# A two-direction GRU kernel: where the row-or-column order of the input is selected, on VectorE or on GpSimd

## The reference

```python
idx = jnp.argmax(probs, axis=-1)
seq_h = xn.reshape(Bx, Hx * Wx, C)
seq_v = jnp.swapaxes(xn, 1, 2).reshape(Bx, Hx * Wx, C)
seq = jnp.where((idx == 1)[:, None, None], seq_v, seq_h)
z = seq @ in_w.T + in_b
yf = _gru_dir(z @ gru_wih_f.T + gru_bih_f, gru_whh_f, gru_bhh_f, False)
yb = _gru_dir(z @ gru_wih_b.T + gru_bih_b, gru_whh_b, gru_bhh_b, True)
y = jnp.concatenate([yf, yb], axis=-1) @ out_w.T + out_b
return x + y.reshape(Bx, Hx, Wx, C)
```

## Time and profile before

| what | value |
|---|---|
| median of 3 runs | 1848.66 us (1848.02 to 1849.3) |
| the profiled execution, its own time | 1848.42 us |
| its span, first to last instruction | 1846.6 us |
| PE busy | 1639.6 us (89%) |
| DVE busy | 1578.8 us (85%) |
| ACT busy | 1227.9 us (66%) |
| POOL busy | 58.2 us (3%) |
| mean granted TensorE clock | 0.516 of full speed |

### The profile page before, as it was taken

One profiled execution on the slowest core, in us unless ns is written; L12 is line 12 of the kernel. 1 busy time (PEld: TensorE's weight loads), 2 busy tenths in 40 slices (PEclk: granted clock), 3 DMA queues, 4 the chain that ended last, 5 costly groups with the idle time before them and its releaser, 6 DMA issues.

```text
span 1846.6 us, 65131 instructions
## 1 busy us (share of the span) xinstructions
PE 1639.6 (89%) x21315; PEld 1240.3 (67%) x21315; DVE 1578.8 (85%) x9056; ACT 1227.9 (66%) x6271; POOL 58.2 (3%) x131
## 2 busy tenths in 40 slices
PE   3558999999999999999999999999999999999997
PEld 2436777676777777777777777776777777777775
DVE  7879888888888888888888888888888888888887
ACT  7935666666666666666666666666666666666665
POOL 5520000000000000000000000000000000000000
PEclk9655555555555555555555555555555555555555
DMA  5200000000000000000000000000000000000000
GB/s 157 69 7 8 13 11 14 11 14 11 13 11 12 12 11 14 10 14 11 13 11 8 11 14 11 12 12 12 12 12 12 11 14 11 13 11 12 12 12 15
DMA packets 40132, 31.27 MB, mean 17 GB/s; under 512 B 3448, under 2 KB 37624, under 8 KB 39800
## 3 DMA queue, kind: packets, MB, share of 16 engines
q1 hardware_dynamic: 39800, 27.13, 5.1%
HBM read 18.73 MB, written 8.39 MB: 15 GB/s over the span
## 4 chain that ended last, share of the span: by engine, by line
PE 56%; DVE 22%; ACT 14%; issue 7%; DMA 0%; POOL 0%; SPq 0%; DVEq 0%; ACTq 0%; POOLq 0%
PE bank L592 56%; DVE state L888 8%; DVE bank L876 8%; ACT rec L496 7%; DVE halves L897 4%; ACT rpair L490 3%; ACT big L432 2%; ACT seq L428 1%; ACT xin L416 1%; DMA gamma_row<-in_gamma 0%; DVE seq L851 0%; DVE rec L903 0%; DVE big L867 0%; ACT zquad L493 0%; DVE xin L821 0%
## 5 line engine op out<-in xcount | busy, mean ns | idle before, releaser
L592 PEld LDWEIGHTS bank<-halves,wsplit 128*128 128x128 f16 x18432 | 697.8, 106 | 504.4 <-DVE halves L897 376.7
L592 PE MATMUL bank<-halves,wsplit 128*128 128x16 f16 x18432 | 883.6, 182 | 133.2 <-DVE halves L897 118.6
L888 DVE TENSOR_TENSOR_SCAN state<-zquad,rec 128x64 f32<-128x64 f32 x2048 | 596.2, 291 | 177.0 <-ACT rec L496 135.1
L592 PE MATMUL bank<-seq,wcomb 128*128 128x128 f32 x1536 | 593.0, 491 | 0.4 <-DVE seq L851 0.4
L496 ACT ACTIVATE rec<-bank 128x16 f32<-128x16 f32 x2048 | 406.5, 198 | 276.4 <-DVE bank L876 81.4
L490 ACT ACTIVATE rpair<-bank 128x16 f32<-128x16 f32 x2048 | 378.9, 185 | 285.7 <-PE bank L592 267.9
L897 DVE SCALAR_TENSOR_TENSOR halves<-state 128x32 f16<-128x32 f32 x2048 | 433.1, 211 | 34.8
L876 DVE TENSOR_TENSOR_SCAN bank<-rpair,bank 128x32 f32<-128x32 f32 x2048 | 440.5, 215 | 22.3 <-ACT rpair L490 6.2
L493 ACT ACTIVATE zquad<-bank 128x16 f32<-128x16 f32 x2048 | 407.6, 199 | 25.1
L592 PEld LDWEIGHTS bank<-seq,wcomb 128*128 128x128 f32 x1536 | 385.9, 312 | 1.3 <-DVE seq L851 1.3
L903 DVE TENSOR_TENSOR rec<-state,signs 128x32 f32<-128x32 f32 x2047 | 370.9, 181 | 3.0
(11 more groups left out here) (118 smaller groups left out, 204.8 us busy)
## 6 DMA issues: line engine op xcount, KB each, us to landing
xin<-in_x SPq DMA_DIRECT2D x16, 512.0 KB, 3.7
big<-in_x SPq DMA_DIRECT2D x128, 64.0 KB
out<-big SPq DMA_DIRECT2D x128, 64.0 KB
wih<-in_wiht SPq DMA_DIRECT2D x2, 384.0 KB
con<-in_consts SPq DMA_DIRECT2D x1, 424.0 KB, 5.3
whh<-in_whht SPq DMA_DIRECT2D x2, 192.0 KB
inw<-in_in_w SPq DMA_DIRECT2D x1, 128.0 KB
outw<-in_outwt SPq DMA_DIRECT2D x2, 64.0 KB
```

The lines of the kernel that those rows point to most:

```text
L592: return nc.tensor.matmul(o, w, m, start=start, stop=True, skip_group_check=True)
L888: v.tensor_tensor_scan(state[:, d, ring, :], zquad[:, e, cols], rec[:, e, cols], 0.0, ALU.mult, ALU.add).then_inc(state_ready[d], 1)
```

## The change

The first and last 16 positions (`EDGE`) are still selected by DVE ahead of the recurrence. All other positions are now handled by POOL, in 31 pairs of chunks (`NCHUNK`), each pair being 16 positions from the start and 16 from the end, in the order in which the recurrence takes them. POOL has no masked copy here: it multiplies `seq` by (1 - mask) and `seq_v` by mask, and then adds the two, so that a pair of chunks takes four multiplies and two adds of 128 x 256 f32 elements, all inputs and outputs in SBUF. The weights stand in a new tensor `choice`, which two small DVE instructions fill behind `mask`; `choice_set` tells POOL. Each add raises `select_rest` by one. PE waits for `select_rest` ahead of the first input fill of every second block, from block 2 to block 62, and SP ahead of the loads of each ring. The 16 selects in the first ring go.

```diff
--- before.py
+++ after.py
@@ -28,7 +28,9 @@
 RING = 2 * TB
 COLS = 2 * B
 TPP = L // P
-EDGE = 4 * TB
+EDGE = 2 * TB
+CHUNK = 2 * TB
+NCHUNK = (L // 2 - EDGE) // CHUNK
 SLOTS = 4
 JA = 2
 K = 2.0 ** 12
@@ -164,6 +166,7 @@
     lg = sb("lg", [B, 16])
     diag = sb("diag", [B, B])
     mask = sb("mask", [P, B], I32)
+    choice = sb("choice", [P, 2, B])
 
     state = sb("state", [P, 2, RING + 1, 4 * B])
     rec = sb("rec", [P, 2, 4 * COLS])
@@ -189,6 +192,7 @@
     xhat_act = sem("xhat_act")
     xhat_pool = sem("xhat_pool")
     gray_sum = sem("gray_sum")
+    choice_set = sem("choice_set")
     select_rest = sem("select_rest")
     fold_set = sem("fold_set")
     link_g = sem("link_g")
@@ -317,8 +321,8 @@
 
         load_tiles(0, 0, None)
         load_tiles(1, 1, None)
-        sp.wait_ge(select_rest, 1)
         for i in range(1, NBLK // 4):
+            sp.wait_ge(select_rest, 2 * i)
             for q in range(2):
                 load_tiles(i * 2 + q, q, i * 4 + (2 * q - 2))
 
@@ -400,6 +404,28 @@
         link(g.tensor_copy(parts[0], w_all))
         g.tensor_scalar(parts[2], parts[0], -1.0, None, ALU.mult)
         g.tensor_tensor(parts[1], w_all, parts[0], ALU.subtract).then_inc(weights_set, 1)
+
+
+        def weighed(t, t0, which):
+
+            part = t[:, t0:t0 + CHUNK, :]
+            weight = choice[:, which, :].unsqueeze(1).to_broadcast([P, CHUNK, B])
+            return g.tensor_tensor(part, part, weight, ALU.mult)
+
+        def chosen(t0):
+            part = seq[:, t0:t0 + CHUNK, :]
+            return g.tensor_tensor(part, part, seq_v[:, t0:t0 + CHUNK, :], ALU.add)
+
+        g.wait_ge(choice_set, 1)
+        for c in range(NCHUNK):
+            ends = (EDGE + c * CHUNK, L - EDGE - (c + 1) * CHUNK)
+            for t0 in ends:
+                for t, which in ((seq, 0), (seq_v, 1)):
+                    links[0] += 1
+                    weighed(t, t0, which).then_inc(link_g, 1)
+            g.wait_ge(link_g, links[0])
+            for t0 in ends:
+                chosen(t0).then_inc(select_rest, 1)
 
 
     @block.scalar
@@ -619,6 +645,8 @@
 
         FILL_BIAS = [G_R, G_Z, G_HN, G_N, None, None, None, None]
         FILL_INPUT = [None, None, (G_R, 0), (G_Z, 0), (G_R, 1), (G_N, 0), (G_Z, 1), (G_N, 1)]
+        FIRST_INPUT = 2
+
         def project(q, d):
 
             h = state[:, d, q * TB:(q + 1) * TB, :].rearrange("p s (b k) -> p (s b) k", k=4)[:, :, 2]
@@ -673,7 +701,10 @@
                 if s == 1 and done >= 0:
                     project(1 - q, 1)
                 if filling and FILL_INPUT[s] is not None:
-                    fill_input(1 - q, kblk + (q + 1), *FILL_INPUT[s])
+                    nxt = kblk + (q + 1)
+                    if s == FIRST_INPUT and EDGE // TB <= nxt < NBLK // 2 and nxt % 2 == 0:
+                        pe.wait_ge(select_rest, nxt)
+                    fill_input(1 - q, nxt, *FILL_INPUT[s])
 
         pe.wait_ge(bias_rows, 1)
         pe.wait_ge(cast_set, 2)
@@ -686,9 +717,7 @@
             fill_input(0, 0, g, 0)
         for g in (G_R, G_N, G_Z):
             fill_input(0, 0, g, 1)
-        body(0, 0)
-        pe.wait_ge(select_rest, 1)
-        for i in range(1, L // RING - 1):
+        for i in range(L // RING - 1):
             body(i * RING, i * 2)
         body(L - RING, NBLK - 2, last=True)
 
@@ -844,6 +873,8 @@
         v.tensor_scalar(diag[:, :], con[0:B, C_IDENT:C_IDENT + B], lg[:, 7:8], None, ALU.mult).then_inc(diag_set, 1)
         dve.wait_ge(mask_mm, 1)
         link(v.tensor_copy(mask[:, :], bank[7][:, 0:B]))
+        v.tensor_scalar(choice[:, 0, :], mask[:, :], -1.0, 1.0, ALU.mult, ALU.add)
+        v.tensor_copy(choice[:, 1, :], mask[:, :]).then_inc(choice_set, 1)
         dve.wait_ge(seq_set, 2 * B)
 
         def select(t0, t1):
@@ -905,7 +936,6 @@
                             signs[:, 0:2 * B].rearrange("p (n k) -> p n k", k=2), ALU.mult).then_inc(rec_ready[d], 1)
 
         def body(base, kblk, first):
-            share = (L - 2 * EDGE) // RING
             for r in range(RING):
                 q, s = r // TB, r % TB
                 candidate(base, r, 0)
@@ -913,10 +943,6 @@
                     record_state((r - 1) % RING, 1)
                 if s in (5, 7) and kblk + q > 0:
                     add_output(kblk + q - 1, (s - 5) // 2)
-                if first:
-                    ins = select(EDGE + r * share, EDGE + (r + 1) * share)
-                    if r == RING - 1:
-                        ins.then_inc(select_rest, 1)
                 new_state(base, r, 0)
                 candidate(base, r, 1)
                 split_state(base, r, 0)
```

## The result

The changed kernel takes 1908.31 us (median of 6 runs, 1907.82 to 1911.65), the kernel before 1848.62 us (median of 6, 1847.7 to 1849.3). The ratio is 1.0328, with a 95% interval from 1.0315 to 1.0341: slower by 60 us, where 1881 us was forecast, in a range of 1845 to 1932 us.

The account below looks back on a forecast made before the run. It took a loop of waits among PE, DVE and ACT, no engine alone, to bound the kernel. From 1848.4 us, less 12.0 and 0.4, plus 45 for POOL holding DVE off, came 1881 us, range 1845 to 1932.

Parts of the forecast that it names:

- What goes: First ring of the recurrence: removing DVE's 16 large selects saves 12.0 us; changes ahead of the recurrence save another 0.4.
- POOL's duration: POOL's 186 two-input instructions of 256 elements: 0.67 us each, 125 us in all.
- The rival of slow shapes: POOL's instructions with the repeated weight row: if over 4.4 us each, PE would wait in each ring; chance 0.05.
- What POOL does to DVE: Recurrence: each POOL instruction's reads hold DVE's two-SBUF-input instructions off for 0.41 us, at 0.81 ns an element; 45 us added.
- POOL's wait of 0.20 us for DVE: Recurrence: each POOL instruction waits 0.20 us for the DVE instruction in front, so POOL does one in 0.87 us.
- the forecast's own formula: DVE's step beside POOL: T = 1.44 + 0.8 x 0.41 x T / 0.87, giving 2.31 us over 70 steps.
- The ratio of 0.62: First ring: DVE work put into a step comes through at 12.0 / 19.5 of its length; applied to POOL's holds, 47 us.
- The rival of the whole instruction: Recurrence: POOL holds DVE off for its whole 0.67 us, adding 90 us, 1926 us in all; chance 0.13.
- The forecast's own case: Recurrence: only POOL's reads hold DVE off, 1881 us, between 1862 and 1905 us; chance 0.60.
- The short hold: Recurrence: POOL holds DVE off only briefly, adding 10 us, 1846 us in all; chance 0.10.
- the clean gain: Recurrence: no contention, DVE's small instructions slip in between POOL's reads and POOL alone waits, 1836 us; chance 0.12.
- The signs named: Trace: POOL busy until some 280 us, four to five rings of about 37 us, two-input DVE groups longer, candidate at 0.2.

Follow-up runs that it names:

- the scratch tensor: Changed kernel with POOL's 186 two-input instructions moved to a tensor no other engine touches, nobody waiting for them, inner positions left unselected: 1909.53 us.
- the paced kernel: Changed kernel with each POOL instruction held back until the forward direction's new state of the next step, one per step for 186 steps: 1906.16 us.

## Why the prediction was right, and where it was off

**What goes.** Forecast 12.4 us. The kernel without POOL's work gains 16 us (13 to 19 us by its interval), 0.76 us of the difference being the part of the first select ahead of the first new state, and 2.8 us lying in the later rings for a reason that is open. The mechanism held for the large selects. The ratio was a little too low: since the first select stands ahead of that ring, it holds 15 and not 16 of them, and 12.0 / 18.3 = 0.66. As a rule for DVE work put into a step, 0.62 fails: pieces of 0.3 us came through at 0.1 to 0.15 of their length in the wait for tanh and at 0.6 ahead of the halves.

**POOL's duration.** Forecast 0.67 us an instruction and 125 us in all; measured 0.72 us each, 0.68 from start to start, and 128.5 us busy. The broadcast weight costs nothing that can be seen, since the adds without it take 723 ns and the multiplies 727. The rival of slow shapes is out.

**What POOL does to DVE.** The forecast was right about which instructions exclude each other: those with two SBUF inputs on DVE, and those alone, are longer, and there is no wait for POOL. It was wrong about how long. The step that failed is "The delay is 0.62 us for 768 elements, 0.81 ns an element", from which it took a hold of 0.41 us for the reads alone. A delay is not a hold. In that pair the DVE multiply started at 103.60, when the cast of 103.08 had already run for 0.52 us, so that the cast held DVE for at least 0.52 + 0.62 = 1.14 of its 1.28 us. The row that spoke against a hold to the end, L399, is a scalar multiplication, and these let go early; the change uses two-input instructions, and no row shows one of them beside a two-input instruction of DVE. Measured, they hold until they end, for 0.72 us, and delay DVE by up to 0.57.

The second term that failed is POOL's wait of 0.20 us for DVE. It measured nothing: POOL starts one instruction every 0.68 us. With 0.57 and 0.68 in the forecast's own formula, T = 1.44 / (1 - 0.8 x 0.57 / 0.68) = 4.4 us over 29 steps, and the added time 79 us; measured were 4.18 us and, in the two slow rings, 66.90 + 62.17 - 2 x 26.72 = 76 us. The ratio of 0.62 that seemed to confirm 45 us did so by chance.

The GPSIMD Engine Reference of the Trainium skill (section 3.1) gives 2.6 cycles an element for a two-input instruction; at its 1.2 GHz that is an estimate of 2.17 ns, and the longest delays with 128 to 512 elements give 2.1. Used for the hold, it would have brought the forecast close.

**The rival of the whole instruction.** This was the right one for the kernel at hand, and the forecast had given it 0.13. It put it at 1926 us because it reckoned with POOL's wait of 0.20 us. With each of a step's six DVE instructions waiting for one of POOL's every 0.68 us, its sum is 31 x (6 x 0.68 - 1.67) = 75 us, and the time 1848.4 - 12.4 + 75 = 1911 us, where 1908 was measured. The forecast's own case had bounds of 1862 and 1905 and missed it; the range held because it took in the rival. For scalar multiplications the rival is wrong, with a loss of 11 us where it has 108. The rule of the Trainium skill (SBUF — State Buffer, "Who interferes with whom") thus agrees with these runs on who excludes whom, down to the POOL that only writes, and on how long for two-input instructions and copies; it differs for scalar multiplications, which hold for some 0.4 of their 0.85 us.

**The other rivals.** The short hold and the clean gain are out. For the clean gain I held that no row showed a scan beside POOL; the new state's scan is delayed too, by up to 0.57 us. That POOL lost more than DVE beside it in the preparation turned round in the recurrence.

**The signs named.** POOL was busy to 248.7 us, against "some 280", and the slow rings were two of 62 to 67 us, not four to five of 37. The forecast had said that rings of 60 us would mean the whole instruction. The candidate stayed at 0.2 us.

## What to carry to other kernels

An engine that is idle is not free: ask which of its instructions read SBUF with two inputs, and how many instructions with two SBUF inputs on VectorE lie on the path beside it. Here each of the latter waited for the end of one of the former, so that 128 us of work of an idle engine cost 77 us, and smaller or paced instructions only lowered that. To read such a hold off a trace, compare where the delayed instruction ends with where the other one ends; how much longer it took depends on when it happened to start. Work of DVE itself, cut into pieces of 0.3 us or less and put where its order already waits, cost 3 to 6 us for all of the selection.

## What the runs showed of the hardware that was not expected

- GpSimd running back to back is not delayed by VectorE here, and VectorE always is. In the recurrence POOL's two-input instructions take 713 to 732 ns (on the scratch tensor 6 of 186 took 0.81 us), while each of DVE's waits for one and then ends within 0.15 us of its end, beside the next one of POOL. In the paced kernel most of POOL's take 0.76 us, 0.04 more; why was not looked into.
- How long a GpSimd instruction of 256 elements holds VectorE off depends on its kind: a multiply or add of two inputs to its end (0.72 us), a copy to its end (0.40 us), a scalar multiplication for some 0.4 of its 0.85 us, a memset (0.31 us) not at all.
- GpSimd's memset of 256 elements, 186 of them back to back, leaves VectorE's two-input instructions as they are: 292 ns against 291.
- The preparation of the same code ends anywhere between 112.6 and 118.4 us in single executions. From a single execution, the rings' lengths tell more than the total. What in the preparation varies was not looked into.
